# Where an expert's weight conversion stands among the row copies of a fused attention and mixture-of-experts layer

## The reference

```python
logits = x @ wg.T                                  # 32 experts
scores = jax.nn.softmax(logits, axis=-1)
weights, idx = jax.lax.top_k(scores, 8)
weights = weights / jnp.sum(weights, axis=-1, keepdims=True)
...                                                # rows sorted by expert: xs, group_sizes
g = jax.lax.ragged_dot(xs, w1, group_sizes)        # 512 -> 192
u = jax.lax.ragged_dot(xs, v1, group_sizes)
h = jax.nn.silu(g) * u
ys = jax.lax.ragged_dot(h, w2, group_sizes)        # 192 -> 512
out = jnp.zeros((T, x.shape[1]), x.dtype).at[t_s].add(ys * w_s[:, None])
```

## Time and profile before

| what | value |
|---|---|
| median of 3 runs | 2560.15 us (2555.6 to 2566.59) |
| profiled execution | 2557.8 us, its span 2556.1 us |
| busy: TensorE, VectorE, ScalarE, GpSimd | 2252.4, 1459.7, 1223.2, 951.0 us |
| share of the span | 88%, 57%, 48%, 37% |
| TensorE's granted clock, mean | 0.946 of full speed |
| DMA over the span | 139 GB/s |

### The profile page before, as it was taken

One profiled execution on the slowest core, in us unless ns is written; L12 is line 12 of the kernel. 1 busy time (PEld: TensorE's weight loads), 2 busy tenths in 40 slices (PEclk: granted clock), 3 DMA queues, 4 the chain that ended last, 5 costly groups with the idle time before them and its releaser, 6 DMA issues.

```text
span 2556.1 us, 61763 instructions
## 1 busy us (share of the span) xinstructions
PE 2252.4 (88%) x11800; PEld 1933.4 (76%) x11801; DVE 1459.7 (57%) x4810; ACT 1223.2 (48%) x2634; POOL 951.0 (37%) x1126
## 2 busy tenths in 40 slices
PE   7999899999989999982899889978999898988990
PEld 5887588888868888861788778867889787977980
DVE  4455567777767777763445444454444545455446
ACT  3343556666656666541344444444444444444443
POOL 1112025555535555554233333322334232423342
PEclk9999999999999999995999999989999899999995
DMA  3334113332333333335997777777777777877778
GB/s 116 91 112 118 58 34 126 107 126 104 129 124 122 117 116 121 108 115 184 252 250 164 150 154 139 137 169 150 144 145 136 163 149 154 141 157 157 137 127 288
DMA packets 164556, 357.25 MB, mean 140 GB/s; under 512 B 21136, under 2 KB 21136, under 8 KB 164368
## 3 DMA queue, kind: packets, MB, share of 16 engines
q0 software_dynamic: 60224, 144.21, 28.4%
q1 hardware_dynamic: 90832, 173.04, 22.8%
q10 hardware_dynamic: 13440, 39.33, 4.8%
HBM read 177.37 MB, written 179.14 MB: 139 GB/s over the span
## 4 chain that ended last, share of the span: by engine, by line
PE 28%; DMA 9%; issue 6%; DVE 4%; ACTq 2%; DVEq 2%; ACT 2%; POOL 1%; POOLq 0%; SPq 0%
DMA moe_sum<-X,aidx 8%; PE bank L438 5%; PE bank L439 5%; PE bank L440 5%; PE bank L429 3%; DVE WB L661 2%; PE bank L455 2%; PE bank L456 2%; PE bank L457 2%; PE bank L459 2%; PE bank L458 2%; PE bank L448 2%; ACTq L318 1%; DVEq L298 1%; ACT BIG L562 1%
## 5 line engine op out<-in xcount | busy, mean ns | idle before, releaser
L1415 POOL DMA_INDIRECT moe_sum<-X,aidx x274 | 426.6, 1557 | 878.0 <-issue 542.2
L438 PE MATMUL bank<-WB,XL 128*128 x1096 | 409.1, 373 | 120.9 <-DVE XL L673 120.5
L895 PE MATMUL bank<-WB,XH 128*128 128x512 f32 x1536 | 478.8, 393 | 0.0
L439 PE MATMUL bank<-WB,XH 128*128 x1096 | 383.4, 350 | 0.0
L440 PE MATMUL bank<-WB,XH 128*128 x1096 | 383.0, 349 | 0.0
L895 PEld LDWEIGHTS bank<-WB,XH 128*128 128x128 f32 x1536 | 290.7, 189 | 60.1 <-issue 0.5
L895 PE MATMUL bank<-WB,XL 128*128 128x512 f32 x768 | 316.3, 412 | 10.6 <-DVE XL L1202 10.6
L895 PE MATMUL bank<-WB,SH 128*128 128x512 f32 x1024 | 319.0, 393 | 0.0
L438 PEld LDWEIGHTS bank<-WB,XL 128*128 128x128 f32 x1096 | 218.6, 199 | 129.7 <-issue 129.6
L1481 POOL DMA_INDIRECT sorted_rows<-srow,pos x256 | 266.1, 1040 | 95.2 <-issue 95.2
L681 DVE SCALAR_TENSOR_TENSOR BIG<-BIG,bank x274 | 95.3, 348 | 345.2 <-ACT BIG L504 332.0
(11 more groups left out here) (202 smaller groups left out, 4220.1 us busy)
## 6 DMA issues: line engine op xcount, KB each, us to landing
BIG<-sorted_rows SPq DMA_DIRECT2D x275, 274.0 KB
X<-x_in SPq DMA_DIRECT2D x64, 256.0 KB, 2.8
RAW<-w_in ACTq DMA_DIRECT2D x15, 768.0 KB, 4.9
LATE<-w_in ACTq DMA_DIRECT2D x15, 768.0 KB, 4.6
sorted_rows<-BIG SPq DMA_DIRECT2D x33, 274.0 KB, 3.3
moe_sum<-LATE SPq DMA_DIRECT2D x34, 256.0 KB, 3.0
LATE<-x_in SPq DMA_DIRECT2D x32, 256.0 KB, 3.1
RAW<-wo_in SPq DMA_DIRECT2D x16, 512.0 KB, 3.5
```

What stands on the lines that cost most here:

```text
L438: nc.tensor.matmul(eu[s][:, 0:UP], XL[:, s, k, :], wh, start=k == 0, stop=False)
L439: nc.tensor.matmul(eu[s][:, 0:UP], XH[:, s, k, :], wh, start=False, stop=False)
L895: last = nc.tensor.matmul(ps, w, m, start=start and i == 0, stop=stop and i == len(terms) - 1)
L1415: nc.gpsimd.indirect_dma_start(acc_dram[:, :], bass.IndirectOffsetOnAxis(aidx[:, s:s + 1], 0), rows, None, compute_op=ALU.add).then_inc(s_ ...
```

## The change

On ScalarE and VectorE the inner step is rotated: it ends with the copy of the rows of tile g+2, where it began with that of tile g+1. The copy for tile 1 stands before the loop. The conversion for expert e+2 (convert) moves from behind the inner loop of expert e to ahead of it, so it follows the copy for the expert's second tile. It writes a set which expert e-2 used, so ScalarE first waits for the last down product of expert e-2 (s_D); the number to wait for is read from a fourth row of the table. The loads for expert e+3 are issued one by one behind the first four pieces. VectorE converts expert 0 ahead of making the tables. SP loads and TensorE transposes one tile more at the end.

The diff; left out is the old place of weights_low, which has moved unchanged:

```diff
--- before.py
+++ after.py
@@ -157,7 +157,7 @@
         AT, ES = MAX_TILES + 2, 4 * EXPERTS
         tn = bq[:, 0:ES].rearrange("p (i n) -> p i n", i=4)
         step = bq[:, ES:ES + 2 * EXPERTS].rearrange("p (i n) -> p i n", i=2)
-        table = bq[0:1, 2 * ES:2 * ES + 3 * EXPERTS].bitcast(i32).rearrange("p (i n) -> p i n", i=3)
+        table = bq[0:1, 2 * ES:2 * ES + 4 * EXPERTS].bitcast(i32).rearrange("p (i n) -> p i n", i=4)
         pair_n = bq[0:1, 3 * ES:3 * ES + 1].bitcast(i32)
         listed = bq[:, 3 * ES + 2:3 * ES + 2 + 2 * TILES // 4].rearrange("p (k j) -> p k j", j=2)
         at_listed = bq[:, 3 * ES + 32:3 * ES + 32 + TILES // 4]
@@ -289,13 +289,14 @@
             return not isinstance(t, int) or 0 <= t - lag < TILES
 
 
-        def each_expert(eng, body):
+        def each_expert(eng, convert, body):
 
             eng.wait_ge(s_tabd, 1)
 
             def one(e, q):
                 n = eng.value_load(table[0:1, 0, bass.ds(e, 1)], min_val=1, max_val=TOKENS // P + 1)
                 first = eng.value_load(table[0:1, 1, bass.ds(e, 1)], min_val=0, max_val=MAX_TILES)
+                convert(e, q)
                 body(e, q, first, n)
                 return first + n
 
@@ -310,13 +311,16 @@
 
             return bass.ds(parity * size + base, n)
 
-        def load_weights(eng, e, i):
+        def load_weights(eng, e, i, part=None):
             to = raws[i]
-            eng.dma_start(to[:, 0:W13], w13_in[bass.ds(e, 1), :, :].rearrange("a p n -> p (a n)")).then_inc(s_ewr[i], 16)
-            eng.dma_start(to[:, W13:W13 + HID], w2_in[bass.ds(e, 1), 0:P, :].rearrange("a p n -> p (a n)")).then_inc(s_ewr[i], 16)
+            if part in (None, 0):
+                eng.dma_start(to[:, 0:W13], w13_in[bass.ds(e, 1), :, :].rearrange("a p n -> p (a n)")).then_inc(s_ewr[i], 16)
+            if part in (None, 1):
+                eng.dma_start(to[:, W13:W13 + HID], w2_in[bass.ds(e, 1), 0:P, :].rearrange("a p n -> p (a n)")).then_inc(s_ewr[i], 16)
             for h in range(2):
-                eng.dma_start(to[h * 64:(h + 1) * 64, W13 + HID:RAW_N],
-                              w2_in[bass.ds(e, 1), P:FFN, :].rearrange("a p n -> p (a n)")).then_inc(s_ewr[i], 16)
+                if part in (None, 2 + h):
+                    eng.dma_start(to[h * 64:(h + 1) * 64, W13 + HID:RAW_N],
+                                  w2_in[bass.ds(e, 1), P:FFN, :].rearrange("a p n -> p (a n)")).then_inc(s_ewr[i], 16)
 
         def moe_sp(sp):
             def fill_pads(e, i):
@@ -376,7 +380,8 @@
             total = sp.value_load(pair_n[0:1, 0:1], min_val=TOKENS * TOP_K // P // 2, max_val=PAGES // 2)
             with sp.Fori(EXPERTS // 2 - 1, total) as p:
                 pair(p)
-            load_rows(2 * total, 0)
+            for s in range(2):
+                load_rows(2 * total + s, s)
             pairs = sp.value_load(pair_n[0:1, 0:1], min_val=TOKENS * TOP_K // P // 2, max_val=PAGES // 2)
             for i in range(2):
                 sp.wait_ge(s_add[i], 16 * pairs + 16)
@@ -478,6 +483,7 @@
                     down(g - 2, s, before)
 
             total = 2 * pairs
+            rows_t(total + 1, 1, pairs)
             act_t(total - 1, 1)
             down(total - 2, 0, slot_at(total))
             down(total - 1, 1, slot_at(total + 1))
@@ -518,34 +524,45 @@
             act.wait_ge(s_ex, TILES)
             nc.scalar.activation(negmax[:, :], mhalf[:, :], ACT.Silu)
             act.wait_ge(s_q, 4 * TILES)
-            for e in range(2):
-                for piece in range(len(PIECES)):
-                    weights_high(e, e, e, piece)
+            for piece in range(len(PIECES)):
+                weights_high(0, 0, 0, piece)
             act.wait_ge(s_elo, 1)
             load_weights(act, 2, 0)
+            for piece in range(len(PIECES)):
+                weights_high(1, 1, 1, piece)
             act.wait_ge(s_T, 3)
             nc.scalar.activation(XHF[:, 0:HID], PS[:, ET:ET + HID], ACT.Copy).then_inc(s_exh, 1)
+            act.wait_ge(s_T, 4)
+            nc.scalar.activation(XHF[:, HID:2 * HID], PS[:, ET + HID:ET + 2 * HID], ACT.Copy).then_inc(s_exh, 1)
+
+            def convert(e, q):
+                if isinstance(e, int) and e + 2 >= EXPERTS:
+                    return
+                load = not (isinstance(e, int) and e + 3 >= EXPERTS)
+                before = act.value_load(table[0:1, 3, bass.ds(e, 1)], min_val=1, max_val=MAX_TILES + 3)
+                act.wait_ge(s_D, before)
+                stand(act)
+                if load:
+                    act.wait_ge(s_elo, e + 2)
+                    stand(act)
+                for piece in range(len(PIECES)):
+                    weights_high(e + 2, (q + 2) % WSETS, q % 2, piece)
+                    if load and piece < 4:
+                        load_weights(act, e + 3, (q + 1) % 2, piece)
 
             def body(e, q, first, n):
                 def tile(g):
                     same = g & 1
                     other = (g + 1) & 1
-                    rows_high(g + 1, other)
                     silu(g, same)
                     act_high(g - 1, other)
                     evacuate(g - 2, same)
+                    rows_high(g + 2, same)
 
                 with act.Fori(0, n) as i:
                     tile(first + i)
-                if not (isinstance(e, int) and e + 3 >= EXPERTS):
-                    act.wait_ge(s_elo, e + 2)
-                    stand(act)
-                    load_weights(act, e + 3, (q + 1) % 2)
-                if not (isinstance(e, int) and e + 2 >= EXPERTS):
-                    for piece in range(len(PIECES)):
-                        weights_high(e + 2, (q + 2) % WSETS, q % 2, piece)
-
-            total = each_expert(act, body)
+
+            total = each_expert(act, convert, body)
             act_high(total - 1, 1)
             evacuate(total - 2, 0)
             evacuate(total - 1, 1)
@@ -567,6 +584,24 @@
 
             dve.wait_ge(s_rk, 2 * TILES)
             dve.wait_ge(s_posf, TILES)
+            def weights_low(e, q, i, piece):
+                dve.wait_ge(s_ehi, len(PIECES) * e + piece + 1)
+                w = WB[:, q * WSET:(q + 1) * WSET]
+                src, n = PIECES[piece]
+                if src < W13:
+                    low, high, rows = w[:, W13 + src:W13 + src + n], w[:, src:src + n], slice(0, P)
+                elif src == W13:
+                    low, high, rows = w[:, W2L:W2L + n], w[:, W2H:W2H + n], slice(0, P)
+                else:
+
+                    low, high, rows = w[64:P, W2X:W2X + n], w[64:P, W2X:W2X + n], slice(64, P)
+                last = nc.vector.tensor_tensor(low, raws[i][rows, src:src + n], high.bitcast(f32), ALU.subtract)
+                if piece + 1 == len(PIECES):
+                    last.then_inc(s_elo, 1)
+
+            for piece in range(len(PIECES)):
+                weights_low(0, 0, 0, piece)
+
             tab = [0]
 
             def done(inst):
@@ -608,6 +643,8 @@
             done(nc.vector.tensor_tensor(tn[:, 2, EXPERTS - 1:EXPERTS], tn[:, 2, EXPERTS - 1:EXPERTS], odd[:, 1:2], ALU.add))
             settled()
             nc.vector.tensor_copy(table[:, 0:2, :], tn[0:1, 2:4, :])
+            nc.vector.memset(table[:, 3, 0:1], 1)
+            nc.vector.tensor_scalar(table[:, 3, 1:EXPERTS], tn[0:1, 3, 0:EXPERTS - 1], 3.0, None, ALU.add)
             nc.vector.tensor_copy(pair_n[:, :], odd[0:1, 2:3]).then_inc(s_tabd, 1)
             for i, (which, src) in enumerate(((ident[:, 0:EXPERTS], step[:, 0, :]), (ident[:, 0:EXPERTS], step[:, 1, :]), (fours, tn[:, 3, :]),
                                               (ident[:, 0:EXPERTS], iota_e[:, :]))):
...
@@ -695,30 +717,35 @@
                 dve.wait_ge(s_yf, g + 3)
                 nc.vector.tensor_copy(aidx[:, at(0, parity, 1, 1)], BIG[:, bass.ds(tail_at(g) + (WR + ID_COL - W_COL), 1)]).then_inc(s_aid, 1)
 
-            for e in range(2):
+            for piece in range(len(PIECES)):
+                weights_low(1, 1, 1, piece)
+            for i in range(2):
+                dve.wait_ge(s_T, 3 + i)
+                nc.vector.tensor_copy(BIG[:, WR + i * TAIL:WR + (i + 1) * TAIL], BIG[:, XR + i * ROW + W_COL:XR + (i + 1) * ROW]).then_inc(s_wr, 1)
+                dve.wait_ge(s_exh, 1 + i)
+                half = slice(i * HID, (i + 1) * HID)
+                nc.vector.tensor_tensor(XLF[:, half], PS[:, ET + i * HID:ET + (i + 1) * HID], XHF[:, half].bitcast(f32),
+                                        ALU.subtract).then_inc(s_exl, 1)
+
+            def convert(e, q):
+                if isinstance(e, int) and e + 2 >= EXPERTS:
+                    return
                 for piece in range(len(PIECES)):
-                    weights_low(e, e, e, piece)
-            dve.wait_ge(s_T, 3)
-            nc.vector.tensor_copy(BIG[:, WR:WR + TAIL], BIG[:, XR + W_COL:XR + ROW]).then_inc(s_wr, 1)
-            dve.wait_ge(s_exh, 1)
```

(11 more changed lines are left out.)

13 lines of the change are left out of this document (removed).

## The result

| kernel | median (lowest to highest) | span, clock of the profiled execution |
|---|---|---|
| before | 2560.14 us (2555.6 to 2566.59, 4 runs) | 2556.1 us, 0.946 |
| changed | 2531.86 us (2529.37 to 2534.86, 4 runs) | 2530.7 us, 0.954 |

The ratio is 0.9888, 95% interval 0.9864 to 0.9912. The change gains 28 us where 73 were predicted, and 2531.86 lies above the range of 2455 to 2528. Lines have moved: L429 is now L434, L438 to L440 are L443 to L445, L448 is L453, L673 is L695, L684 is L706, L494 is L500.

A forecast was written before the change was run, and what follows sets the result against it. Bound: TensorE's stalls at changes of expert, chiefly 120.5 us waiting for the rows' low half, plus the clock falling behind them. Terms -88 + 5 + 10 + 0 = -73 us gave 2487 us, range 2455 to 2528.

The forecast's parts named there:

- plain changes: Changes of expert without single-tile experts: 18 stalls of 6.9 us fall to 2.0 each, 88 us gained.
- single-tile experts: Six experts with one tile: the second conversion waits for later-issued loads, 8.3 us against 7.5 each, 5 us lost.
- rest of the stage (DMA, adds): Weight loads land under running steps: 0.42 us for one step behind each of 24 changes, 10 us lost.
- set-up: Before the expert stage: VectorE's pieces of expert 0 ahead of the table stay hidden with 2.7 us to spare, 0.
- the first piece starts at t0+3.0: ScalarE at a change, t0 the new expert's first transposes: row copy and three table reads (1.7 us) precede the conversion.
- so at 2.0 the clock loss, 1.7 to 1.8 of each 6.9, goes too: TensorE behind the shortened pause: the clock holds, as after one 2.4 us pause, saving 1.7 to 1.8 us per change.
- one more 0.42 us operation, of which 0.3 shows: Down products behind TensorE's 1.65 us wait need one more operation, adding 0.3 for 2.0 us per plain change.
- A: The stall only moves: 4 us wait at the activation transposes, clock falling, 5.5 us per change; about 2542 us, chance 0.09.
- C: VectorE's pieces hold up GpSimd's row adds, 24 x 1.8 = 43 us lost; 2530 us, chance 0.05.
- D: Slower, the row-add queue becomes the bound: 0.42 us over all 273 steps, about 2592 us, chance 0.04.
- E: No effect: ScalarE waits at s_D or at the table long enough to undo the gain; 2560 us, chance 0.03.
- B: Conversions wholly hidden at a change: stall 0.5 us, adds unhurt, 115 us gained less 5; 2450 us, chance 0.09.

The follow-up runs named there:

- e1: The changed kernel with the four weight loads issued behind the six pieces, not between them; 2514.43 us, ratio to before 0.9822.
- e3: The changed kernel with TensorE's four weight-slot reads at the head of each pair of tiles, not two per tile; 2713.43 us in a single run.
- e8: The changed kernel, each expert's first tile written out, pieces ahead of its row copy, issues last, TensorE's second slot read behind the up products; 2523.16 us.
- e11: The changed kernel, each expert's first tile written out, all six pieces behind its row copy, issues last, third table read gone; 2520.85 us.
- e13: e11 with every weight load from the third expert on cut to 16 columns; 2479.09 us in a single run.
- e17: e14 with VectorE's last two pieces moved behind the next expert's first low rows, its first tile written out for this; 2503.36 us.
- e9: The changed kernel, each expert's first tile written out, two pieces each behind activation copy, eviction and row copy, issues last; 2528.47 us.
- e10: The kernel before with only the four weight-load issues moved behind the six pieces; 2506.6 us.
- e14: e10 with the first tile's number counted in a register on ScalarE and VectorE, not read from the table; 2494.29 us, ratio 0.9733.
- e16: The kernel before, issues ahead of the pieces, with every weight load from the third expert on cut to 16 columns; 2554.68 us, single run.
- e12: e10 with every weight load from the third expert on cut to 16 columns; 2492.72 us in a single run.

## Why the prediction was wrong

The sum, set against the traces. The step times give 17 plain changes in the changed kernel (the step with the pause and the next), where I had 18:

| term | predicted | measured |
|---|---|---|
| plain changes | 124 to 36, -88 us | 124 to 82.0 (4.8 each), -42 us |
| single-tile experts | 45 to 50, +5 | 49.6 to 54.6, +5 |
| rest of the stage (DMA, adds) | +10 | +8 |
| set-up | 0 | +3.4 |

(The 54.6 us are summed over three steps at each of the six places; the 45 of the prediction counted one step, and the same three steps hold 49.6 in before.) The measured terms add up, but for rounding, to the 25.4 us between the two profiled spans.

**Plain changes, 2.0 us each.** This is the step that failed. It misses 46 us, as much as the whole sum does. Over the two steps at each of the 17 places:

| us per plain change | before | predicted | changed | e1 |
|---|---|---|---|---|
| pause | 4.97 | 1.65 | 2.46 | 1.85 |
| lost by the lower clock | 2.08 | 0 | 1.60 | 0.38 |
| waits ahead of the row transposes | 0 | 0 | 0.27 | 0.65 |
| in none of these | 0.09 | 0.3 | 0.50 | 0.72 |
| sum | 7.14 | 2.0 | 4.82 | 3.59 |

The second row is the share of the clock that was not granted, summed over the time in which TensorE does not wait.

(1) *"the first piece starts at t0+3.0"*: it starts at t0+3.8 (t0 = 1581.11). I took 0.29 us for a read; the first of the three takes longer in the changed kernel, as its line 297 shows against the earlier trace rows:

```profile
L297 ACTq TENSOR_LOAD <-bq x32: 277/668/975, 1220.0 to 2374.8; - x32
```

Over 0.5 us were 17 of these 32, in before 2. In both kernels an ACTIVATE is running when this read starts, a piece there and the row copy here, so why it takes longer stays open. Pieces and issues took 3.8 us for my 3.5. So the pause shown above is 2.66 us for 1.65.

(2) *"so at 2.0 the clock loss, 1.7 to 1.8 of each 6.9, goes too"*: this is the largest part. The loss is 1.6 us a change, three quarters of what it was. I relied on one pause of 2.4 us that kept the clock. Of the pauses over 0.6 us, 21 of 33 have a mean clock under 0.97 in the four microseconds behind them (before 23 of 30), and behind this 2.66 us pause it stays at 0.50 through the next row transposes.

(3) *"one more 0.42 us operation, of which 0.3 shows"*: it is 0.5, and 0.3 of waits ahead of the transposes come on top. Those are mostly TensorE's own reads (20.3 us in 39 gaps over the stage, before 6.5 in 19; e3 moved them and they grew, e8 took one away and they halved).

The pause of 2.4 us in the step from 2360.99 had more to say than I read in it. It is the one stall of before with no issues ahead of its pieces, since no weights are left to load:

```profile
2357.54 0.60 ACT L515 ACTIVATE X<-bank  x1 [0.78 <-POOLq L781]
2358.04 2.79 ACT L494 ACTIVATE WB<-LATE 128x384 fp32r<-128x384 f32 x6
...
2364.05 0.43 PE L438 MATMUL bank<-WB,XL 128*128 x1 [2.43 <-DVE XL L673]
```

Its step lost 2.8 us where the other plain ones lost 7.1; from the evacuation ahead of the pieces to the first up product it takes 6.5 us, at 1435 it takes 9.3. That is one case and not a clean one (ScalarE also waits for an output buffer just ahead), but it pointed at the issues before any run did.

**The mechanism credited with the gain was the wrong one.** The prediction gave the whole -4.9 us per change to the rows standing ahead of the pieces. In its working the mixing was hidden: 2.4 and 2.81 us in a row became 3.5, 1.7 us a change. The runs show that this part alone is worth 27 us in the order of before, and that the rows-last order alone loses 15.6. The reordering moves XH and a third read into the same chain: with the issues ahead, 113.0 us of waits at L453 stand for 120.5 at L438, and a pause of 4.3 us for one of 5.0. Its other costs are the gaps ahead of the transposes, the excess away from changes (27.8 us, before 21.4), the later start of the stage, and single-tile experts.

**Single-tile experts**: as forecast, 5 us in all, 9.1 us each for 8.3 (I had 8.3 for 7.5). **DMA and adds**: 8 us for 10, of which 6.4 lie away from the changes; that transfers are the cause was not tested. The pauses also stayed; e11, e13 and e17 show that the row loads behind the weights are the next bound once the pause is under 2 us. **Set-up**: judged hidden, it costs 3.4 us of start (1218.68 for 1215.32). VectorE's earlier pieces were hidden, but the load for expert 2 is now issued earlier, and the page list, asked for 1.7 us sooner, lands at 1200.88 for 1198.54. That the load delays it is borne out by e13, which has this set-up with that load cut small: the list lands 11.2 us after it was asked for, 15.6 us in e11 with the load in full, 15.8 in the changed kernel and 11.8 in before. One profile with the load in full, e9's, has 12.1, so it does not always happen.

**The rivals.** A, "the stall only moves", had the time nearest to the result (2542) and a chance of 0.09. Its reason was half right: table reads cost more and the clock falls, but issue and pieces do overlap. C is refuted: the row add L1442 has a mean of 1551 ns. D and E did not come. B's short pause nearly came in e11 (0.9 us at a plain change), in a kernel of 2520.85 us, so it would not have given 2450: there the excess at a plain change is still 4.6, of which 2.3 are waits ahead of the row transposes, 1.8 of them for rows. With the small loads of e13 it is 3.7, and some 1.4 to 1.5 us in either kernel are in no wait; only 0.3 to 0.4 of that is the clock, and what the rest is stays open. The range was too narrow above, since it priced pauses up to 3.0 us at little more than their own length.

## What to carry to other kernels

Where an engine's queue issues DMAs next to work of its own, put the issues behind instructions that are ready to run: a four-line move of the issues (e10) gains 2.1%, more than the whole change, and one table read less brings it to 2.7% (e14). When an edit carries two changes, price each alone: I had both numbers in one term and gave the credit to the wrong one. One pause that kept the clock is no price for the next: count how many of the pauses of that length kept it. A pause that is cut short uncovers the transfers that it hid, so look at the DMA share in the microseconds behind it before counting the gain.

## What the runs showed of the hardware

- ScalarE's queue hands out six pieces and goes on to DMA issues while they run: four issues of 0.34 to 0.55 us each lengthen the pieces by nothing there (2.80 us in e10, 2.81 in before). Between the pieces they stretch them to 3.80 us. With nothing handed out they cost some 1.8 to 2.1 us at each of 29 places (53.5 us in before against e10, 62 in e16 against e12).
- A read of a register from the table has a median of 0.28 to 0.29 us on ScalarE in before and in the second and third read of the changed kernel, but 0.67, at most 0.98, in its first (L297), which starts beside the row copy; on TensorE, four reads in a row leave gaps of 1.75 us (233.4 us in 133).
- With 1.3 MB of weights just issued, the row loads that TensorE waited for in e11 landed 6.3 to 9.6 us after their issue (15 of them); with small loads the waits for rows fell from 34.4 to 3.0 us.
- Pauses near 2.5 us on TensorE came both with a clock that stayed at 1.00 and with one that fell to 0.50 for several microseconds, in the same kernel. In the changed one, these are the four microseconds behind a pause of 2.47 us and behind one of 2.48 us (clock third from the end):

```profile
1362.76:1366.76 4.00, 3.34 (x17) 2.57 (x18) 2.08 (x6) 1.33 (x3) 1.55 (x1) 1.00 0.84 192
1643.03:1647.03 4.00, 3.61 (x13) 2.57 (x14) 2.39 (x9) 1.25 (x3) 1.55 (x1) 0.68 0.77 178
```
